# Second and third layer norm moved into the second attention, and two weight loads moved ahead, in a four-layer transformer kernel on one core

## The reference

```python
x = ln(x + attention_with_relative_positions(x))     # 16 heads of 8
x = ln(x + six_local_layers(x))                      # each: windowed attention (16 heads of 64, window 32),
                                                     # then a gated FFN; tokens are shifted before both
x = ln(x + causal_attention(x))                      # 16 heads of 8, Wqkv, bqkv, Wout, bout
x = ln(x + experts(x))                               # 8 experts of 64, top 2 of a softmax gate, token by token
```

```python
qkv = x @ Wqkv + bqkv
scores = einsum('bthd,bshd->bhts', q, k / sqrt(8)) + triu(-10000, 1)
out = softmax(scores) @ v  ->  (b, s, 128) @ Wout + bout
```

## Time and profile before

| what | us |
|---|---|
| three timed executions | 5344.72, 5363.97, 5366.69 (median 5363.97) |
| the profiled execution | 5351.69 |
| its span (page's first line) | 5349.9 |
| first norm (1205 to 1240) | 35 |
| second norm and set-up, to the first transposition | 34.4 |
| second attention, to its last residual | 622.5 |
| from there to the first gates of the experts | 12.8 |
| from the first gates to the end | 140.0 |

### The profile page before, as it was taken

How to read it: one execution, slowest core, us unless ns; L and a number is a source line. 1 busy time by engine, 2 the same in 40 slices (tenths; PEclk the granted TensorE clock), 3 DMA queues, 4 the chain that set the end, 5 groups by cost and what they waited for, 6 DMA issues and landing times. The chain is left out here.

```text
span 5349.9 us, 207782 instructions
## 1 busy us (share of the span) xinstructions
PE 4868.3 (91%) x85362; PEld 4041.8 (76%) x85362; DVE 3833.0 (72%) x7728; ACT 3248.1 (61%) x6115; POOL 3414.8 (64%) x2162
## 2 busy tenths in 40 slices
PE   6999999985999999999999999999999997688879
PEld 5888888874888788877887788778877886355557
DVE  4777777756888778877887788778877886554543
ACT  2333333324777777777777777777777775466654
POOL 1111111107999989999999899989998995221212
PEclk9999999997999999999999999999999998798889
DMA  1000000002322232223222322232222221000000
GB/s 44 6 6 6 6 6 6 6 19 69 81 69 68 71 82 69 69 71 83 69 68 69 85 68 68 72 82 68 68 71 71 68 69 42 4 0 0 0 5 17
DMA packets 418171, 253.89 MB, mean 47 GB/s; under 512 B 200288, under 2 KB 413822, under 8 KB 416911
## 3 DMA queue, kind: packets, MB, share of 16 engines
q1 hardware_dynamic: 412464, 235.42, 18.2%
q10 hardware_dynamic: 5344, 12.98, 0.8%
HBM read 25.07 MB, written 4.25 MB: 5 GB/s over the span
## 5 line engine op out<-in xcount | busy, mean ns | idle before, releaser
L1213 POOL TENSOR_TENSOR b_rnorm<-b_ss,neghalf 128x16 f32<-128x16 f32 x384 | 1117.8, 2911 | 35.7 <-DVE b_ss L1721 34.7
L1209 POOL TENSOR_TENSOR b_rot<-b_t 128x1024 f32<-128x1024 f32 x384 | 908.7, 2366 | 97.9 <-DVE b_t L1710 94.6
L1708 DVE TENSOR_TENSOR b_t<-psum,b_cosg 128x1024 f32<-128x1024 f32 x384 | 469.3, 1222 | 480.0 <-ACT b_sq L1577 474.0
L1218 POOL TENSOR_TENSOR b_qk<-b_rot,b_rnorm 128x1024 f32<-128x1024 f32 x384 | 731.0, 1904 | 55.1
L1324 PE MATMUL psum<-b_w_hi,b_xT_parts 128*128 128x512 f32 x1152 | 527.4, 458 | 28.3 <-issue 17.9
L379 POOL TENSOR_TENSOR a_k_diag<-a_k_parts,a_head_rows 128x1024 fp32r<-128x1024 f32 x64 | 119.8, 1894 | 651.3 <-PE psum L516 602.9
L1577 ACT ACTIVATE b_sq<-psum 128x1024 f32<-128x1024 f32 x384 | 391.7, 1020 | 236.6 <-PE psum L1329 236.3
L1715 DVE TENSOR_REDUCE b_ss_floor<-b_sq 128x16 f32<-128x1024 f32 x384 | 463.8, 1208 | 0.0
L1329 PE MATMUL psum<-b_w_hi,b_xT_parts 128*128 128x512 f32 x1152 | 458.6, 398 | 0.0
L1325 PE MATMUL psum<-b_w_lo,b_xT_parts 128*128 128x512 f32 x1152 | 457.3, 397 | 0.0
L1411 PE MATMUL psum<-b_wo,b_oT 128*128 128x128 f32 x3072 | 425.3, 281 | 0.8 <-ACT b_oT L1595 0.8
(11 more groups left out here) (249 smaller groups left out, 12046.1 us busy)
## 6 DMA issues: line engine op xcount, KB each, us to landing
b_v_win<-b_v SPq DMA_DIRECT2D x2304, 65.0 KB
b_v_win<-b_v SPq DMA_DIRECT2D x1152, 32.5 KB
oa<-XR SPq DMA_DIRECT2D x1024, 2.0 KB
xcur<-X SPq DMA_DIRECT2D x111, 128.0 KB, 4.7
b_wqkv<-in_L_ffn_Wqkv_dram ACTq DMA_DIRECT2D x6, 1536.0 KB
b_x_shifted<-X SPq DMA_DIRECT2D x96, 64.0 KB
b_x_shifted<-X SPq DMA_DIRECT2D x96, 63.5 KB
b_wo<-in_L_ffn_Wo_dram SPq DMA_DIRECT2D x12, 256.0 KB, 3.0
```

Source lines behind the costliest of these rows:

```text
L1209: nc.gpsimd.tensor_tensor(rot[:, i, :, :], t1[:, i, :, :], t2[:, i, :, :], ALU.add).then_inc(rot_done, 1)
L1213: nc.gpsimd.tensor_tensor(rnorm[:, i, :], ss[:, i, :], neghalf[:, :], ALU.pow).then_inc(rn_done, 1)
L1218: nc.gpsimd.tensor_tensor(qk[:, i, :, :], rot[:, i, :, :], rnorm[:, i, :, None].broadcast_to((P, 16, BD)), ALU.mult).then_inc(qk_done, 1)
L1708: nc.vector.tensor_tensor(t14, x4, tab(cosg, slice(0, BD), BD), ALU.mult)
```

## The change

1. `layer_norm("ln2")` and the set-up block are gone. In the attention, `statistics(n)` on DVE adds the residual of one sequence and takes its moments, `scales(n)` on POOL computes `rstd` and `shift`, `normalised(n)` on ACT writes the two tiles back to `X`. Sequences 0 and 1 are done in part `first`; the others in the loop: statistics at the end of slots 0 and 8, `normalised` at the end of slots 3 and 11, `scales(n)` in POOL's queue ahead of the diagonals of sequence n - 1, `copy_x(n)` behind them.
2. The repeated weights, `bias_k`, `ident80` and `mask_in` are made on ACT at the start of part `first`, `vones` and `mask_all` on POOL. `copy_x` is a multiply by ones in place of a copy.
3. SP issues all 22 loads (14 of the attention, 8 of the experts) between `shift_x(94)` and `shift_x(95)`. The tiles are allocated for the whole rest of the program.
4. Third norm: `statistics3(0)` and `(1)` on DVE at the end of slots 0 and 10 of part `last`, `scales3(0)` and `(1)` on POOL behind its last diagonals, `normalise3(0)` on ACT, two tiles at the end of each of slots 6 to 9. Only `normalise3(1)` of the first two groups stays in the experts' block.

The diff, cut to its core (semaphores and tile declarations, renamings and the removed copies of moved lines are left out):

```diff
+        def statistics3(dve, g):
+            for t in range(GD):
+                nc.vector.bn_stats(stats3[:, t, :], X[:, g * GD + t, :]).then_inc(moments3_ok, 1)
+            if g > 0:
+                dve.wait_ge(x3_ok, g * GD)
+            dve.wait_ge(moments3_ok, (2 * g + 1) * GD)
+            for t in range(GD):
+                nc.vector.bn_aggr(mv3[:, t, :], stats3[:, t, :]).then_inc(moments3_ok, 1)
+            dve.wait_ge(moments3_ok, (2 * g + 2) * GD)
+            nc.vector.tensor_scalar(var3[:, :], mv3[:, :, 1], EPS, None, ALU.add).then_inc(var3_ok, 1)
+            nc.vector.tensor_scalar(less_mean3[:, :], mv3[:, :, 0], -1.0, None, ALU.mult).then_inc(var3_ok, 1)
+        def scales3(pool, g):
+            pool.wait_ge(var3_ok, 2 * g + 2)
+            nc.gpsimd.tensor_tensor(rstd3[:, :], var3[:, :], neghalf[:, 0:GD], ALU.pow).then_inc(rstd3_ok, 1)
+            pool.wait_ge(rstd3_ok, g + 1)
+            nc.gpsimd.tensor_tensor(shift3[:, :], less_mean3[:, :], rstd3[:, :], ALU.mult).then_inc(shift3_ok, 1)
+        def normalise3(act, g, tiles=range(GD)):
+            act.wait_ge(shift3_ok, g + 1)
+            for t in tiles:
+                x = X[:, g * GD + t, :]
+                nc.scalar.activation(x, x, ACT.Identity, bias=shift3[:, t:t + 1],
+                                     scale=rstd3[:, t:t + 1]).then_inc(x3_ok, 1)
+                    def load_second_layer():
...
+                        sp.dma_start(wqkv_c[:, :], T["L1_attn_Wqkv"]).then_inc(c_ld2, 16)
+                        sp.dma_start(wout_c[:, :], T["L1_attn_Wout"]).then_inc(c_ld2, 16)
...
+                        sp.dma_start(gate_w[:, :], T["L1_ffn_gate_w"]).then_inc(d_ld, 16)
+                        sp.dma_start(lower[:, :, :].rearrange("p a c -> p (a c)"), T["lower"]).then_inc(d_ld, 16)
...
                     shift_x(DEPTH * B - 2, B - 2)
+                    load_second_layer()
                     shift_x(DEPTH * B - 1, B - 1)
...
-        layer_norm("ln2", residual=XR)
...
-                    with pool.Fori(0, B // 2) as b:
-                        for q in range(2):
-                            nc.gpsimd.tensor_copy(xcur[:, :, :],
-                                                  X[:, bass.ds(b * 2 * LT + q * LT, LT), :]).then_inc(x_copied, 1)
+                    def scales(n):
+                        pool.wait_ge(var_ok, 2 * n + 2)
+                        if not isinstance(n, int) or n > 0:
+                            pool.wait_ge(x_ok, LT * n)
+                        nc.gpsimd.tensor_tensor(rstd[:, :], var[:, :], neghalf[:, 0:LT], ALU.pow).then_inc(rstd_ok, 1)
+                        pool.wait_ge(rstd_ok, n + 1)
+                        nc.gpsimd.tensor_tensor(shift[:, :], less_mean[:, :], rstd[:, :], ALU.mult).then_inc(shift_ok, 1)
+                    def copy_x(n):
+                        pool.wait_ge(x_ok, LT * n + LT)
+                        nc.gpsimd.tensor_tensor(xcur[:, :, :], X[:, bass.ds(n * LT, LT), :],
+                                                ones[:, 0:1, None].broadcast_to((P, LT, D)), ALU.mult).then_inc(x_copied, 1)
+                    def diagonals(n, q):
                             for hq in range(NG):
-                                pool.wait_ge(k_ok, (b * 2 + q) * 2 + hq // 2 + 1)
+                                pool.wait_ge(k_ok, n * 2 + hq // 2 + 1)
                                 nc.gpsimd.tensor_tensor(k_diag[:, q, hq * 4:hq * 4 + 4, :],
                                                         k_parts[:, hq:hq + 1, :].bitcast(F32).broadcast_to((P, 4, S)),
-                                                        head_rows[:, :, None].broadcast_to((P, 4, S)),
+                                                        head_rows_c[:, :, None].broadcast_to((P, 4, S)),
                                                         ALU.mult).then_inc(diag_ok, 1)
+                    nc.gpsimd.memset(vones[:, :, :, :, :], 1.0).then_inc(set_c, 1)
+                    nc.gpsimd.memset(mask_all[:, :], -125.0).then_inc(set_c, 1)
+                    scales(0)
+                    scales(1)
+                    copy_x(0)
+                    diagonals(0, 0)
+                    copy_x(1)
+                    with pool.Fori(0, B // 2 - 1) as b:
+                        for q in range(2):
+                            scales(b * 2 + 2 + q)
+                            diagonals(b * 2 + 1 + q, 1 - q)
+                            copy_x(b * 2 + 2 + q)
+                    diagonals(B - 1, 1)
+                    scales3(pool, 0)
+                    scales3(pool, 1)
...
+                        def normalised(n):
+                            act.wait_ge(shift_ok, n + 1)
+                            for t in range(LT):
+                                x = X[:, bass.ds(n * LT + t, 1), :].rearrange("p a c -> p (a c)")
+                                nc.scalar.activation(x, x, ACT.Identity, bias=shift[:, t:t + 1],
+                                                     scale=rstd[:, t:t + 1]).then_inc(x_ok, 1)
                         if part == "first":
+                            act.wait_ge(c_ld2, 16 * N_C)
+                            for t, rep in ((1, wk_rep_c), (0, wq_rep_c)):
+                                w = wqkv_c[:, t * D:(t + 1) * D].rearrange("p (g c) -> p g c", g=NG)[:, :, None, :]
+                                nc.scalar.mul(rep[:, :, :, :], w.broadcast_to((P, NG, 4, GC)),
+                                              SCALE_A if t else 1.0).then_inc(set_c, 1)
+                            nc.scalar.mul(bias_k[:, :], bias_k0[:, :], SCALE_A).then_inc(set_c, 1)
+                            nc.scalar.mul(ident80[:, :], ident[:, :], 80.0).then_inc(set_c, 1)
+                            nc.scalar.copy(mask_in[:, :], mask0[:, :]).then_inc(set_c, 1)
+                            normalised(0)
+                            normalised(1)
+                            act.wait_ge(set_c, 7)
...
+                            if part == "loop" and j in (3, 11):
+                                normalised(b * 2 + (2 if j == 3 else 3))
+                            if part == "last" and j in (6, 7, 8, 9):
+                                normalise3(act, 0, range(2 * j - 12, 2 * j - 10))
...
+                        def statistics(n):
+                            tiles = X[:, bass.ds(n * LT, LT), :]
+                            nc.vector.tensor_tensor(tiles, tiles, XR[:, bass.ds(n * LT, LT), :], ALU.add).then_inc(moments_ok, 1)
+                            dve.wait_ge(moments_ok, n * MOM + 1)
+                            nc.vector.memset(pause[:, :], 0.0)
+                            for t in range(LT):
+                                nc.vector.bn_stats(stats[:, t, :], X[:, bass.ds(n * LT + t, 1), :]
+                                                   .rearrange("p a c -> p (a c)")).then_inc(moments_ok, 1)
+                            dve.wait_ge(moments_ok, n * MOM + 1 + LT)
+                            nc.vector.memset(pause[:, :], 0.0)
+                            for t in range(LT):
+                                nc.vector.bn_aggr(mv[:, t, :], stats[:, t, :]).then_inc(moments_ok, 1)
+                            if not isinstance(n, int) or n > 0:
+                                dve.wait_ge(shift_ok, n)
+                            dve.wait_ge(moments_ok, n * MOM + MOM)
+                            nc.vector.tensor_scalar(var[:, :], mv[:, :, 1], EPS, None, ALU.add).then_inc(var_ok, 1)
+                            nc.vector.tensor_scalar(less_mean[:, :], mv[:, :, 0], -1.0, None, ALU.mult).then_inc(var_ok, 1)
                         if part == "first":
+                            statistics(0)
+                            statistics(1)
+                            dve.wait_ge(set_c, 7)
...
+                            if part == "loop" and j in (0, 8):
+                                statistics(b * 2 + (2 if j == 0 else 3))
+                            if part == "last" and j in (0, 10):
+                                statistics3(dve, j // 10)
...
+                    pool.wait_ge(d_ld, 16 * N_D)
                     ties(0)
...
+                    act.wait_ge(d_ld, 16 * N_D)
                     turned_x(0)
                     gate_exps(0)
                     gelu(0)
-                    normalise3(1)
+                    normalise3(act, 1)
...
-                    statistics3(0)
-                    statistics3(1)
                     gate_logits(0)
```

More of the change, by code:

```diff
@@ new lines, in build_program @@
+        mask_in, mask_all = sb(ctx, "c_mask_in", [P, P], BF16), sb(ctx, "c_mask_all", [P, P], BF16)
+        ident80 = sb(ctx, "c_ident80", [P, P], BF16)
+        GD, NGRP, SG = 8, NT // 8, 8 // LT
+        gate_w = sb(ctx, "d_gate_w", [P, NEXP])
+        w1_d, b1_d, w2_d = (sb(ctx, n, shape) for n, shape in
+                            (("d_w1", [P, NEXP, EH]), ("d_b1", [P, NPR]), ("d_w2", [P, NPR, D])))
+        b2 = sb(ctx, "d_b2", [NEXP, D])
+        ROWG = (0, 32)
+        rows = sb(ctx, "d_rows", [ROWG[1] + NEXP, NPR, P])
```

(31 more changed lines are left out.)

121 lines of the change are left out of this document (38 added, 83 removed).

## The result

The changed kernel takes 5337.3 us, the median of 20 runs (5328.4 to 5347.3). The kernel before, run beside it, takes 5354.8 (20 runs, 5344.4 to 5367.0). The ratio is 0.9966, 95% interval 0.9958 to 0.9974: 17.6 us less. The profiled execution took 5333.6 us, its span is 5331.8, so again 1.8 us lie outside.

A forecast was written before the change was run, and what follows sets the result against it. In the attention no engine is full; a ring of PE, DVE and ACT steps sets the pace. 28.4 - 13.0 - 2.0 - 2.1 - 0.5 + 9.5 = 20.3 us off 5351.7 gives 5331.4, placed 6 higher: 5337 us, range 5313 to 5363.

The forecast's parts named there:

- Part 1: Second norm and set-up before the first turn_x: 34.4 us removed, 6.0 added, gain 28.4 us (bounds 26 to 31).
- Part 2: The 22 loads on SP between the last two shift_x: cost zero; 7 us if they were twice as slow.
- Part 3: Statistics on DVE in loop slots 0 and 8: exponentials 0.93 us later, 14 times, loss 13.0 us (bounds 0 to 27).
- The slack: In the k1 slot, DVE's maximum can be 0.47 us late before ACT's exponentials become late.
- Parts 4 and 5: In the loop, normalised on ACT (0, at most 1.4 us) and scales and copy_x on POOL (zero, over 3 us to spare).
- Part 6: Third norm's groups 0 and 1 in the attention's last part: losses of 2.0, 2.1 and 0.5 us.
- Part 7: Last residual to the experts' first gates: PE can transpose when the block starts, gain 9.5 us.
- no change of its average: PE's granted clock in the loop: average unchanged; bounds 17 us lost to 40 us won.
- Rival A: Statistics cost nothing in the loop: 5324 us, or 5315 or less with a better clock; chance 0.2.
- B: Rival: PE's low clock spreads to loop sequences that now escape it, 17 us lost, 5354 us; chance 0.17.
- C: Rival: one more low-clock stretch of PE in each loop sequence, 39 us lost, 5376 us; chance 0.06.
- the ring: Attention's pace-setting cycle: PE scores, DVE maximum, ACT exponentials, PE turn, ACT copy, PE outputs and next scores.

The follow-up runs named there:

- e4: Kernel before with only the 22 loads moved between the last two shift_x; 5365.2 us, ratio 1.0005 to before.
- e5: Kernel before plus an unused DVE reduction over 240 columns at the end of loop slots 0 and 8; ratio 1.0006 to before.
- e2: Changed kernel with the loop's statistics moved to slots 3 and 11, normalised to 4 and 12, scales behind the diagonals; 5327.1 us, ratio 0.9931 to before.
- e7: Kernel before plus an unused DVE reduction over 1328 columns at the end of loop slots 3 and 11; ratio 0.9997 to before.
- e9: Kernel before plus an unused DVE reduction over 1432 columns at the end of loop slots 0 and 8; ratio 1.0019 to before.
- e8: Changed kernel with loop and third-norm statistics in slots 3 and 11, loop normalised in 4 and 12, first seam reordered; 5315.0 us, ratio 0.9917 to before.
- e1: Changed kernel without the second norm of sequences 2 to 15, so part of the computation is left out; 5323.9 us, ratio 0.9933 to before.
- e6: Kernel before plus an unused DVE reduction over 1328 columns at the end of loop slots 0 and 8; ratio 0.9990 to before.
- e3: Changed kernel with the third norm's groups 0 and 1 back behind the attention, loads still early; 5333.9 us, ratio 0.9953 to before.
- e12: e8 with the third norm's first two groups back behind the attention; 5323.6 us, ratio 0.9927 to before.

## Why the prediction was right

The forecast was 5337 us against 5337.3, and 20.3 us off before's profiled execution; between the profiled executions it is 18.1, between the medians 17.6, between the means of two spans 20.7. That the time fits to 0.3 us is luck: the forecast started from some 5357.7 for the kernel before, which took 5354.8, 2.9 less, and the gain between the medians is 2.7 less than forecast. Step by step, by the means of the spans:

- *Part 1, gain 28.4.* Measured 29.0. From the block's first instruction to the first transposition 5.56 us were taken (4534.36 to 4539.92) in place of 6.0: power and shift take 0.97, not 1.3. Right.
- *Part 2, loads, zero.* Right by SyncE's queue. The loads alone (e4) shorten both seams but won nothing in all, which the prediction did not foresee. In e4's profile the time was gone before the first load was issued; what took it, the runs do not show.
- *Part 3, statistics in the loop, 13.0.* The mechanism and the place are right. The size is a little off. The maximum comes 1.60 us later, not 1.4 (the statistics take 1.54, and a longer hand-over 0.06), and the exponentials 1.13 later, not 0.93, in every sequence: 15.8 at full clock. Measured over the first 14 periods it is 13 x 0.81 + 2.9 = 13.4, since the mean period grew only from 38.41 to 39.22. The slack is shown by e5, the slot by e2 and e7, and DVE's share alone by e9.
- *Parts 4 and 5, ScalarE and POOL, zero.* Right: the full-clock sequence grew by the 1.13 of DVE's slot and nothing else. In e2 and e8, which do the same work in other slots, the mean periods are 38.51 and 38.25, at before's 38.22 and 38.59.
- *Part 6, third norm, 4.6.* This is the term that was mis-sized. The attention's remaining growth is 22.5 - 13.4 = 9.1. The second group costs 2.1, as forecast: from the last addition of V's bias to the last maximum it is 24.0 us in after, e1 and e2, and 21.9 to 22.3 in every other profile. The tiles on ACT cost nothing: e8 has them too. The first group holds up its maximum by 3.9 us, not 2.5, because one of its small instructions takes 1.40 us, beside POOL's diagonals, and not 0.17; the exponentials behind it come 3.3 later, not 2.0. And what I left out is that a maximum this late lets PE stand still, for 3.4 us in the last k1 slot and for 3.7 at the end, and that PE's clock is low behind both. The last whole period grew from 38.3 to 43.7, which is 2.1 more than the first group's 3.3. The tail takes 12.7 us in both profiles of after, and 12.8 and 13.0 in e1 and e2 with the same slot, where all others lie between 11.1 and 11.8: 1.5 more. 3.3 + 2.1 + 2.1 + 1.5 = 9.0. How much of the first 2.1 is the clock's (0.72 and 0.73 in place of 0.81 and 0.90) and how much the later order of work is not separated. e8 gives period and tail back (38.6 and 11.3).
- *Part 7, second seam, gain 9.5.* Measured 9.9. Right.
- *The clock, "no change of its average".* In the loop 7.7 and 8.7 us of a sequence at 1.2 GHz before, 7.0 and 7.1 after: true in the loop by luck of the length, as e6 and e9 show, and not true in the last part. Rival A did not come (the period would have stayed), and neither did B or C: the mean period grew by 0.8 us, the one at full clock by 1.13. But the way I priced the slot, late time x count, is safe only at a fixed clock: e6 pays that price in every slot and loses nothing.

So two errors cancelled: the last part cost 4.5 us more than forecast, and the untouched stages came out 4.3 lower, which I take as scatter. Without it the gain would have been 20.7 - 4.3 = 16.4 us.

The Trainium skill ("TensorE: Matmul & The Clock Gate", section "A second HAM failure mode: psum-queue depth-cycling") has short idleness of PE swing its clock. The swing is in every trace of this loop. That more idleness makes it worse, as I read it against the change, the runs do not bear out: e6 has about 1 us more of waiting per sequence and less time at the low clock, e9 has 0.12 us more than e6 and again as much low time as before.

## What to carry to other kernels

Price added work by the slot it stands in: what the next step of the ring waits for there, and by how much. Fourteen times 1.54 us cost the changed kernel some 13 us in one slot and next to nothing three slots later: moving the work (e2) won as much as leaving it out (e1). Look for such slots at the end of a stage too, where a stalled PE also loses its clock; and before dropping a part that is worth nothing, ask whether it is only in the wrong place (e3 against e12).

Where PE's clock swings in a loop, the sum of waits is not the time. Repeat the profile, compare sequences at full clock (36.49 and 36.50 us in the two profiles of the changed kernel), and leave the average to timed runs.

## What the runs showed of the hardware

- 0.12 us more per sequence (36.37 to 36.49 at full clock) raised the mean period by 1.0 us, from 38.24 in e6's profile to 39.24 in e9's, and the kernel's time by 0.29% (ratios 0.9990 and 1.0019, intervals apart). The granted clock falls into another order of slow and fast sequences.
- Added waiting can pay for itself: with 1.54 us of useless DVE work per sequence the time at 1.2 GHz fell from 7.7 or 8.7 us to 4.9, and the ratio is 0.9990.
- Around the stall of 3.74 us at the end of the attention the granted clock fell: 0.70 over the 12.7 us from the last maximum on, where the kernel before, whose longest wait there is 1.67 us, has 1.00.
- A small DVE instruction can end with a long one of POOL's. The addition of eps for eight tiles (`d_var`, 128x8) takes 0.17 us where POOL is idle, and 1.40 or 1.41 in the four profiles (after twice, e1, e2) where it starts beside POOL's two diagonals; it ends 0.02 to 0.03 us after them each time. The bn_stats ahead of it, beside the same diagonals, take 1.65 us, and 1.63 to 1.64 where POOL is idle. Why the one waits and the other does not, no run here shows.
